# Loads and stores of the node stages: two queues for the heads' result, GpSimd for the node rows, a divided last table store

## What is computed

```python
h = jnp.maximum(_layernorm(x, axis=-1), 0.0)          # first node stage
x = x + _L0_gnn_ref(h, edge_attr_64, ...)             # two heads; ends in the lines below
    h = ft.mean(axis=1)
    mu = h.mean(axis=0)                               # over all nodes
    var = h.var(axis=0)
    h = (h - mu) / jnp.sqrt(var + BN_EPS) * bn_gamma + bn_beta
    h = jax.nn.relu(h)
h = jnp.maximum(_layernorm(x, axis=-1), 0.0)          # middle part
x = x + _L1_gnn_ref(h, edge_index, ...)               # three layers; each begins with h @ W, h @ W a_src, h @ W a_dst
```

## Time and profile before

| what | us |
|---|---|
| median of 3 runs | 8678.86 (8674.43 to 8679.24) |
| the profiled execution: its time | 8679.17 |
| its span, first to last instruction | 8677.4 |
| first node stage: span's start to the first instruction of the heads layer | 89.4 |
| heads layer | 89.4 to 2235.9 |
| middle part: first issue to the first issue of the next phase | 2235.93 to 2361.19 |
| three plain layers | 2361.2 to 8677.4 |

### The profile page before, as it was taken

How to read it: one execution, slowest core, us unless ns; L and a number is a source line. 1 busy time by engine, 2 the same in 40 slices (tenths; PEclk the granted TensorE clock), 3 DMA queues, 4 the chain that set the end, 5 groups by cost and what they waited for, 6 DMA issues and landing times. The chain is left out here.

```text
span 8677.4 us, 123713 instructions
## 1 busy us (share of the span) xinstructions
PE 4711.8 (54%) x23534; PEld 4272.8 (49%) x23534; DVE 6773.1 (78%) x12836; ACT 4577.6 (53%) x12378; POOL 6319.6 (73%) x6672
## 2 busy tenths in 40 slices
PE   5777777777555545455545555555554444444444
PEld 5666666666344444444444444444444444444444
DVE  6888888888577777777777777777777777777777
ACT  5777777777344444444444444444444444444444
POOL 4777777777177777777767777777776777777776
PEclk8666666666655555555555555555555555555555
DMA  2222222222222222222212222222221222222221
GB/s 76 56 58 58 56 58 58 58 56 59 64 32 32 32 32 32 32 32 32 32 30 32 32 32 32 32 32 32 32 32 31 35 35 35 35 35 35 35 35 32
DMA packets 575997, 348.39 MB, mean 40 GB/s; under 512 B 451469, under 2 KB 452365, under 8 KB 575951
## 3 DMA queue, kind: packets, MB, share of 16 engines
q0 software_dynamic: 212992, 229.61, 16.6%
q1 hardware_dynamic: 362239, 118.14, 5.9%
q10 hardware_dynamic: 720, 0.17, 0.0%
HBM read 319.61 MB, written 27.76 MB: 40 GB/s over the span
## 5 line engine op out<-in xcount | busy, mean ns | idle before, releaser
L1626 POOL DMA_INDIRECT plain_rows_in<-table,plain_idx x4992 | 4713.1, 944 | 1744.0 <-issue 1744.0
L1889 PE MATMUL plain_ps_sums<-plain_rows_in,plain_prob 128*128 x10080 | 2350.3, 418 | 0.0
L1889 PEld LDWEIGHTS plain_ps_sums<-plain_rows_in,plain_prob 128*128 128x128 f32 x10080 | 2229.1, 330 | 53.7 <-issue 0.5
L1034 POOL DMA_INDIRECT heads_rows_in<-h_in,heads_idx x1664 | 1595.8, 959 | 587.3 <-issue 506.9
L1910 PE MATMUL plain_ps_max<-ident,plain_column_max 128*128 128x128 f32 x312 | 148.2, 475 | 2375.2 <-DVE plain_column_max L1743 2375.2
L1814 ACT ACTIVATE plain_ps_score<-plain_mask,plain_rows_in 128x128 f32<-128x128 f32 x3744 | 1134.1, 352 | 422.6 <-DMA plain_rows_in<-table,plain_idx 422.6
L1843 ACT ACTIVATE plain_prob<-plain_prob 128x512 f32<-128x512 f32 x936 | 712.6, 772 | 1144.0 <-DVE plain_prob L1762 1134.2
L1910 PEld LDWEIGHTS plain_ps_max<-ident,plain_column_max 128*128 128x128 f32 x312 | 56.8, 182 | 2467.1 <-DVE plain_column_max L1743 2467.1
L1814 ACT ACTIVATE plain_score_sb<-plain_mask,plain_rows_in 128x128 f32<-128x128 f32 x1248 | 398.3, 389 | 1557.4 <-DMA plain_rows_in<-table,plain_idx 1557.4
L1734 DVE TENSOR_TENSOR plain_top<-plain_score_sb,plain_ps_score 128x512 f32<-128x512 f32 x312 | 214.6, 688 | 983.7 <-ACT plain_ps_score L1814 983.3
L1762 DVE TENSOR_TENSOR plain_prob<-plain_prob,plain_ps_max 128x512 f32<-128x512 f32 x936 | 754.1, 861 | 19.9
(11 more groups left out here) (253 smaller groups left out, 8555.4 us busy)
## 6 DMA issues: line engine op xcount, KB each, us to landing
plain_rows_in<-table,plain_idx POOLq DMA_INDIRECT x4992
heads_edges<-in_edge_attr SPq DMA_DIRECT2D x108, 512.0 KB
heads_rows_in<-h_in,heads_idx POOLq DMA_INDIRECT x1664
plain_own<-table SPq DMA_DIRECT2D x324, 33.5 KB
table<-plain_out_sb SPq DMA_DIRECT2D x208, 33.5 KB
plain_dst_ids<-in_dst SPq DMA_DIRECT2D x324, 8.0 KB
plain_unit_par<-unit_floats SPq DMA_DIRECT2D x324, 1.0 KB
plain_unit_int<-unit_ints SPq DMA_DIRECT2D x324, 0.0 KB
```

Source lines behind the costliest of these rows:

```text
L1034: gp.indirect_dma_start(rows_in[h][:, t, :], None, table[:, :], bass.IndirectOffsetOnAxis(ap=idx[h][:, t:t + 1], axis=0)).then_inc(gathere ...
L1626: gp.indirect_dma_start(rows_in[h][:, t, :], None, table[:, :], bass.IndirectOffsetOnAxis(ap=idx[h][:, t:t + 1], axis=0)).then_inc(gathere ...
L1889: ins = te.matmul(sums[h % 2], prob[h % 2][:, t, :], rows, start=t == 0, stop=t == Q - 1)
```

## The change

- **Loads of the middle part.** Each of the five loads is issued as two, partitions 0 to 63 (LOWER) by SP and partitions 64 to 124 (UPPER) by ScalarE, ahead of its first square. Both raise the chunk's semaphore, and TensorE waits for 32 in place of 16.
- **Node rows.** The five stores of `xs` to `x_rows` move from SP's queue to GpSimd's, with a semaphore of their own; GpSimd waits for all at the end. SP's stores of the table no longer stand behind them.
- **Last store of the table, in both node stages.** The fifth store is divided into three: the first 12 blocks of all 125 partitions, issued by SP when group 23 of 25 is done; and the last 8 blocks, when all are done, LOWER by SP and UPPER by ScalarE.

```diff
                 def load_half(eng, lanes):
+                    for c in range(chunks):
+                        eng.dma_start(hs[lanes, self.cols(c), :], by_node(h_rows)[lanes, self.cols(c), :]
+                                      ).then_inc(h_loaded[c], 16)
...
                 def _(sp):
+                    load_half(sp, LOWER)
+                    sp.wait_ge(ones_made, 1)
+                    for c in range(chunks - 1):
+                        sp.wait_ge(products_scaled, of_chunk * (c + 1))
+                        store_table(sp, slice(0, ROWS), self.cols(c), stored)
+                    sp.wait_ge(products_scaled, groups - LAST_GROUPS)
+                    store_table(sp, slice(0, ROWS), slice(self.cols(chunks - 1).start, last_blocks.start), stored)
+                    sp.wait_ge(products_scaled, groups)
+                    store_table(sp, LOWER, last_blocks, stored)
+                    sp.wait_ge(stored, 16 * (chunks + 1))
+                    sp.wait_ge(stored_upper, 16)
...
+                @block.gpsimd
+                def _(gp):
                     for c in range(chunks):
-                        sp.dma_start(hs[:, self.cols(c), :], by_node(h_rows)[:, self.cols(c), :]
-                                     ).then_inc(h_loaded[c], 16)
...
+                        gp.wait_ge(mid_made, c + 1)
+                        gp.dma_start(by_node(x_rows)[:, self.cols(c), :], xs[:, self.cols(c), :]
+                                     ).then_inc(mid_stored, 16)
+                    gp.wait_ge(mid_stored, 16 * chunks)
...
+                    load_half(ac, UPPER)
                     for c in range(chunks):
                         square(c, hs, spread, squared)
...
+                    ac.wait_ge(products_scaled, groups)
+                    store_table(ac, UPPER, last_blocks, stored_upper)
...
-                        te.wait_ge(h_loaded[c], 16)
+                        te.wait_ge(h_loaded[c], 32)
```

In the first node stage:

```diff
+    def store_last(self, sp):
+
+        blocks = self.cols(self.chunks - 1)
+        sp.wait_ge(self.rows_copied, self.chunks)
+        sp.wait_ge(self.products_copied, self.groups - 2)
+        self.store_rows(sp, slice(0, ROWS), slice(blocks.start, blocks.stop - 2 * GROUP), self.stored)
+        sp.wait_ge(self.products_copied, self.groups)
+        self.store_rows(sp, slice(0, P // 2), slice(blocks.stop - 2 * GROUP, blocks.stop), self.stored)
+
+    def store_last_upper(self, ac):
+
+        ac.wait_ge(self.products_copied, self.groups)
+        self.store_rows(ac, slice(P // 2, ROWS), slice(self.nb - 2 * GROUP, self.nb), self.stored_upper)
```

More of the change, by code:

```diff
@@ L191, in _ @@
                 sp.dma_start(unit_floats.rearrange("(p c) k -> p c k", p=P), floats[:, :, :]).then_inc(stored, 16)
-                nodes.store(sp, nodes.chunks - 2, nodes.chunks)
+                nodes.store(sp, nodes.chunks - 2, nodes.chunks - 1)
+                nodes.store_last(sp)
                 sp.wait_ge(stored, 32)
@@ L425, in __init__ @@
             sem("n0_stored"))
-        self.rows_copied = sem("n0_rows_copied")
+        self.rows_copied, self.stored_upper = sem("n0_rows_copied"), sem("n0_stored_upper")
     def cols(self, c):
@@ L444, in load_chunk, with store_rows @@
                      self.x.rearrange("(p b) d -> p b d", p=ROWS)[:, self.cols(c), :]).then_inc(self.loaded[c], 16)
+    def store_rows(self, eng, lanes, blocks, done):
+        eng.dma_start(self.table[0:self.x.shape[0], :].rearrange("(p b) d -> p b d", p=ROWS)[lanes, blocks, :],
+                      self.rows_out[lanes, blocks, :]).then_inc(done, 16)
     def store(self, sp, first, last):
@@ L449, in store @@
             sp.wait_ge(self.products_copied, self.of_chunk * (c + 1))
-            sp.dma_start(self.table[0:self.x.shape[0], :].rearrange("(p b) d -> p b d", p=ROWS)[:, self.cols(c), :],
-                         self.rows_out[:, self.cols(c), :]).then_inc(self.stored, 16)
+            self.store_rows(sp, slice(0, ROWS), self.cols(c), self.stored)
+    def store_last(self, sp):
[8 more added lines that the diff above has]
+        self.store_rows(ac, slice(P // 2, ROWS), slice(self.nb - 2 * GROUP, self.nb), self.stored_upper)
     def all_stored(self, sp):
-        sp.wait_ge(self.stored, 16 * self.chunks)
+        sp.wait_ge(self.stored, 16 * (self.chunks + 1))
+        sp.wait_ge(self.stored_upper, 16)
     def extend(self, ve):
@@ L513, in scalar @@
         copy_products(self.groups - 1)
+        self.store_last_upper(ac)
     def tensor(self, te, first, last):
@@ L636, in run, with load_half, store_table @@
                 sem("n1_stored"))
+            stored_upper, mid_stored = sem("n1_stored_upper"), sem("n1_mid_stored")
+            LOWER, UPPER = slice(0, P // 2), slice(P // 2, ROWS)
+            LAST_GROUPS = min(2, of_chunk - 1)
+            last_blocks = slice(nb - LAST_GROUPS * GROUP, nb)
             with nc.Block() as block:
+                def load_half(eng, lanes):
+                    for c in range(chunks):
+                        eng.dma_start(hs[lanes, self.cols(c), :], by_node(h_rows)[lanes, self.cols(c), :]
+                                      ).then_inc(h_loaded[c], 16)
+                def store_table(eng, lanes, blocks, done):
+                    eng.dma_start(by_node(table)[lanes, blocks, :], rows_out[lanes, blocks, :]).then_inc(done, 16)
@@ L639, in _ @@
                 @block.sync
                 def _(sp):
-                    for c in range(chunks):
-                        sp.dma_start(hs[:, self.cols(c), :], by_node(h_rows)[:, self.cols(c), :]
-                                     ).then_inc(h_loaded[c], 16)
[L644 to L650, removed]
@@ L651, in _ @@
-                    sp.wait_ge(stored, 32 * chunks)
+                    load_half(sp, LOWER)
[5 more added lines that the diff above has]
+                    store_table(sp, slice(0, ROWS), slice(self.cols(chunks - 1).start, last_blocks.start), stored)
```

## The result

The changed kernel takes 8720.17 us (median of 6 runs, 8718.78 to 8726.00) against 8678.88 us before: 41.3 us slower, ratio 1.005, 95% interval 1.0038 to 1.0062. The profiled execution is the longest of the six (8726.0, span 8724.2); its extra 5 us lie in the plain layers, which a later run comes back to.

What follows compares the result with a forecast made beforehand. GpSimd's gathers fill the four layers, untouched; the middle part waits for loads on five engines at 132 GB/s. Terms 38.8 + 0.5 - 9.7 + 3.3 = +32.9 us gave 8712, range 8701 to 8725.

Steps and rivals of the forecast that it cites:

- the three counts of small packets: DMA queues: packets of 130, 720 and 479 taken to show 125 rows use 5 engines, 128 use 16, 103 use 1.
- rival 1: Middle part's loads and last stores: UPPER spreads over 16 engines like LOWER; -34 us, 8645; chance 0.09.
- rival 2: Middle part's loads: one engine per UPPER load, but a new one each time; -23 us, 8656; chance 0.04.
- rival 4: Loads and stores: dear and cheap cancel, e.g. two or three engines share 61 rows; no change; chance 0.03.
- rival 3: Middle part's node rows: GpSimd's copies stand on one engine; +33 + 60 us, 8772; chance 0.02.
- Loads: Middle part's start: one engine carries 325 rows where five carried 125 each; last landing +38.8 us, bounds +34.9 to +42.
- The last matmuls: Mean in the middle part: its last six matmuls follow a gap and run at the lower clock; +0.5 us.
- Moves as a block: Middle part after the mean's last matmuls: the same instructions as before, only shifted in time.
- The wait for room: ScalarE's load issues: it may stand there for tens of us, but its first square needs the mean; nothing.
- GpSimd's stores: Node rows in the middle part: GpSimd was idle and its copies are covered by other work; 0.
- End of the middle part: Last product to next phase: mid_x leaves SP's queue earlier, data end sooner; -9.7 us, bounds -5 to -12.
- End of the first stage: Last table store: the busiest engine needs 8.4 us in place of 5.2; +3.3 us, bounds 0 and +5.

Runs made afterwards that it cites:

- e1: The changed kernel with its loads whole again, five of 125 rows on SP's queue; 8679.3 us, against 8678.0 for the kernel before.
- e3: The changed kernel with loads cut at 61, SP loading the first 61 rows and ScalarE the other 64; 8722.6 us, against 8678.0 before.
- e4: The changed kernel with loads and last stores cut at partition 112, both parts of each load issued by SP; 8656.7 us, against 8678.0 before.
- e7: The kernel before, unchanged, run for a second profile; 11735.0 us, in a slow job where before took 11755.6.
- e7b: The kernel before, unchanged, run for a third profile; 8688.7 us, against 8692.7 for before in the same job.
- e5: The kernel before with only the node rows' stores moved to GpSimd; 11788.9 us against 11755.6 in a slow job, the same again 8685.3 against 8692.7.

## Why the prediction was right, and where its sizes were off

- **The engines.** 61 rows on one engine: shown by 310 packets, the share of 0.06, and e1 and e3. The inference from the three counts of small packets before held for a number of rows that the trace before did not have on that queue. Rivals 1, 2 and 4 are out; rival 3, GpSimd's copies on one engine, is out by its 2.6 us a copy. Rivals 1 and 2 also promised too large a gain, since both left out TensorE's own work on the chunks: with data on 16 engines and no gap, e4 starts chunk 4 at 15.3 us, 11.6 sooner than before and not 17.6 (rival 1), and five chunks landing at once near 2251.5 (rival 2) would still have had TensorE's work on all of them (12.7 us in e4) ahead of the mean.
- **Loads, +38.8 us forecast.** Measured +42.3 (26.9 to 69.2), just over the bound of +42. The later chunks are as forecast: 11.91 us apart, 61 rows at 0.195 us. The step that failed is that the engine with UPPER's rows works at full rate from the start: while all 16 engines were at work the total was 207 GB/s, 13 GB/s each and not 26.4, until about 2250, so that engine got half as many rows through in that time. By the packet records a row of 5,120 bytes took 0.40 us between 2244 and 2250 and 0.20 us afterwards. In 6 us at half rate 3 us are lost, an estimate that covers nearly all of the difference of 3.5. The sum charged each row the price it has with five engines at work; no row before showed 16 engines busy with loads of such rows for a stretch.
- **The last matmuls, +0.5 us.** 4.13 us from TensorE's start on chunk 4 to the mean against 3.66: right.
- **"Moves as a block".** From the mean's start to the last product the changed kernel took 1.5 us more (77.1 against 75.6). e7 has 75.4 and e7b 77.1, so before shows both lengths too.
- **The wait for room costs ScalarE nothing.** Its issues took 41.23 us, and its first square started 1.5 us after VectorE's subtraction began, as before. Right.
- **GpSimd's stores, 0.** All five were issued within 0.6 us each, the last at 2376.56, and its data were in by the time the table's last rows were stored. Right, and better than its near row from SP.
- **End of the middle part, -9.7 us.** Measured -7.9 against the first profile, but only -2.8 and -2.2 against the two later ones. Two things were off. The price of the last rows: after 2391 the engine with 61 rows of 2,144 bytes ended 1.7 us later than the byte count gave (its data end at about 2401.1 by the DMA view, 9.5 us after the last product, against 7.8). And the base: I took one execution's late engine for the rule; two further profiles of before do not have it. The prediction named that engine in its bounds, at the new kernel's end only, not at the old one's.
- **End of the first stage, +3.3 us.** Measured +4.3 (8.4 to 12.7, and 12.7 and 13.0 in e1 and e3).
- **Sum, +32.9 us.** By the stretches it is 42.3 + 0.5 + 4.3 less 2.2 to 7.9: +39 to +45, and the medians say +41.3. The range of 8701 to 8725 holds 8720.2, in its upper part, since all three sizes were off to the same side; no error cancelled another.

What the change set out to do was half right. It took SP's backlog away (e5: 5 to 6 us at the end of the middle part), and the limit it went for, the loads, was really there. But the limit was five engines, and the cut at 64 of 125 rows turned five into one for half the data. Cut at 112, the same lines gain.

## What to carry to other kernels

Before dividing a transfer, count the engines that it has now: its completion packets, or the DMA share times 16 when nothing else runs. Then choose the pieces by the largest divisor up to 16 of their row counts, each piece on its own: on the queues of SP and ScalarE 61 rows went to 1 engine here, 125 to 5, 13 to 13, and 64 and 112 to 16. A piece on one engine goes at 26 GB/s, and whoever waits for the whole waits for that piece. Look too at what the next engine needs for its own work; in e4 TensorE no longer waits after chunk 0, so faster loads would gain only as much as chunk 0 came sooner. A store whose end a barrier waits for deserves the same look, and an end read from one profile deserves a second one.

## What was not expected of the hardware

- All 16 engines busy at once carried 207 GB/s with 5,120-byte rows (share 1.01), and 240 to 260 with the cut at 112, where one alone carries 26, and each row took twice as long (0.40 us): the share then tells that engines are occupied, not that they move at full rate.
- The same loads by one queue end 13.5 us after the first issue, by two queues 14.3.
- GpSimd's copy of 125 rows took 2.6 us, at up to 380 GB/s in a slice, against 5.8 us from SP's queue with the same rows.
- The last rows stored by one engine, 61 of 2,144 or 2,176 bytes, ran at 24 to 25 GB/s, somewhat below the 26 of longer rows.
